# GpSimd normalises the softmax rows with one scalar per partition: four operations a step in place of two

## The chip, the core and the metric

The kernel runs on one core of a Trainium2 chip. The metric is the device time of one execution in microseconds (us), the median over several runs. Engines are named as in the profile: PE (TensorE; PEld is its weight load), DVE (VectorE), ACT (ScalarE), POOL (GpSimd) and SP (the queue that issues the DMAs here).

## What is computed

Two residual layers over x of shape (16, 256, 256), 4096 tokens of width 256, in float32.

```
# layer 0: attention, 16 heads of 64, one shared key/value head and one null key
xn = ln(x);  q = l2norm(xn @ Wq) * q_scale;  k = l2norm(xn @ Wk) * k_scale;  v = xn @ Wv
sim = 8 * q @ [k_null, k]^T + [null_bias, rel_pos_bias];  causal and given mask
attn = softmax(sim, axis=-1)          # this division is what the change touches
x = x + ln((attn @ [v_null, v]) @ Wout) * g_out
# layer 1: mixture of experts, 8 routed (best 2 of a softmax) and 2 shared blocks
h_e = leaky(x @ w_gate[e]) * (x @ w_up[e])
x = x + x1_part + sum_e weight_e * (h_e @ w_down[e])
```

## The kernel before

The program is written engine by engine; the order of work on each engine is the order of the code, and semaphores tie the engines together. The 4096 tokens go in eight rounds of 512 (two sequences of 256). Rounds 1 to 6 are one loop body (`Fori`), the first and the last round are written out. In round r the attention of round r is interleaved with the experts of round r-1, so that PE always has matmuls of one or the other.

Attention of a round runs in 16 steps n of two heads each: groups g of four steps, of which each has half the heads of one sequence. For each pair of heads there are two query tiles of 128 rows: tile 1 sees 256 keys and tile 0 sees 128, each with one null key behind them, so the rows in SBUF are `T1[sl]` (257 columns a head) and `T0[sl]` (129 columns a head), with `sl = g % 2`. All of them are parts of one buffer that the profile calls `work`. What one step does, in the order of the data:

- PE, `score` (L1502 to L1519): mask product (L1512) and score products (L1517) into psS.
- DVE, `scores` (L1153 to L1170): adds the bias, writes T1 and T0 and their lowest values (L1161, L1167), and frees psS for the next `score`.
- ACT, `exps` (L752 to L763): exponentials with the row sums `den` (L757, L761).
- DVE, `rdens` (L1140 to L1143): `rden = 1 / den`, one step later in DVE's order.
- POOL, the change (L591 to L595): waits for `rden_done`, multiplies T1's two heads by their reciprocals (L592) and T0's two heads by theirs (L594). Each is one `tensor_tensor` over both heads, the reciprocals read as a second tensor, broadcast along the row. The second one counts `norm_done` up.
- PE, `turn` (L1521 to L1539), three steps behind `score` (`TURN_LAG`): waits for `norm_done`, transposes T1 (L1528) and T0 (L1535) into psT, which ACT (L769) and DVE (L1176) copy out. `value` (L1553, L1556) follows five steps behind.

POOL has other work in the same queue: in eight of the 16 steps `weigh` (L606) multiplies an expert's hidden tile H by its token weights Wb ahead of the step's two operations; at step 9 a small power (L573) for the next round's first layer norm; at the ends of a round powers for other norms (L578, L581, L598).

DVE has two pieces of the next round's layer norm between its steps: at step 8 `norm_stats` (L846, L850, and L853, a `tensor_scalar` of four elements), and at step 11, just behind `rdens(10)`, `norm_x`: four `tensor_scalar` of 128x256 on `xin` (L858), each with a mean and a reciprocal deviation per partition. They stand ahead of `turned` (L1176) and of the next step's `scores`.

`stand` (L95 to L98) puts an instruction of its own behind a wait, so that the wait doesn't sit on the first of several operations.

Of the kernel before, what the change touches and what calls it, by code (L numbers as in the profile page):

```python
# [7 lines left out]
ALU = mybir.AluOpType  # L8
# [9 lines left out]
P = 128  # L18
B, N, D = 16, 256, 256
# [66 lines left out]
def need(eng, ev, r, c):  # L86


    value = ev.at(r, c)
    if isinstance(value, int) and value <= ev.base:  # L90
        return
    eng.wait_ge(ev.sem, value)


def stand(eng, waited):  # L95


    eng.sem_inc(waited, 1)  # L98
# [21 lines left out]
def attention_moe(nc, x, condT, condR, mask, wq, wkv, wout, wgu, wdown, wt, wgT, gnorm,  # L120
# [8 lines left out]
    with ExitStack() as ctx:  # L129
        def sb(name, shape, dt=F32):  # L130
            return ctx.enter_context(nc.sbuf_tensor(name, shape, dt))
# [4 lines left out]
        def events(name, per, base=0):  # L136
            return Events(ctx.enter_context(nc.semaphore(name)), per, base)
# [43 lines left out]
        T1 = [work[:, i * GH * (N + 1):(i + 1) * GH * (N + 1)].rearrange("p (h j) -> p h j", h=GH)  # L181
              for i in range(2)]
        T0 = [work[:, 2 * GH * (N + 1) + i * GH * (P + 1):2 * GH * (N + 1) + (i + 1) * GH * (P + 1)]
              .rearrange("p (h j) -> p h j", h=GH) for i in range(2)]
        low = [sb(f"low{i}", [P, 2, GH]) for i in range(2)]
        den = [sb(f"den{i}", [P, 2, GH]) for i in range(2)]
        rden = [sb(f"rden{i}", [P, 2, GH]) for i in range(2)]
# [199 lines left out]
        norm_done = events("norm_done", ALL)  # L387
# [20 lines left out]
        down_ps = events("down_ps", TILES)  # L408

        waited = ctx.enter_context(nc.semaphore("waited"))  # L410
        waited_sp = ctx.enter_context(nc.semaphore("waited_sp"))
        PRE_SMALL = 16 * 8

# [4 lines left out]
        def scale_q(eng, r, t, done):  # L418

            need(eng, rq_done, r, t + 1)  # L420
            need(eng, qs_done, r, t + 1)
            q3 = qs[t].rearrange("p (h d) -> p h d", h=HEADS)
            eng.tensor_tensor(q3, q3, rq[:, t, :].unsqueeze(2).to_broadcast([P, HEADS, DH]), ALU.mult) \  # L423
                .then_inc(done.sem, 1)
# [126 lines left out]
        @block.gpsimd  # L551
        def _(pool):
            pool.sem_inc(hw_done.sem, hw_done.base)
            pool.memset(ident[:], 0.0).then_inc(pre_p.sem, 1)
            pool.memset(neghalf[:], -0.5).then_inc(pre_p.sem, 1)
            pool.iota(posi[:], pattern=[[-P, 2]], base=N - 1, channel_multiplier=-1).then_inc(pre_p.sem, 1)
            pool.iota(iota8i[:], pattern=[[1, E]], base=0, channel_multiplier=0).then_inc(pre_p.sem, 1)
            pool.wait_ge(pre_p.sem, 4)
            pool.affine_select(out=ident[:], in_=ident[:], compare_op=ALU.not_equal, fill=1.0, base=0,
                               pattern=[[-1, P]], channel_multiplier=1).then_inc(pre_p.sem, 1)  # L560
            pool.wait_ge(pre_p.sem, 5)
            pool.memset(flip[:], 0.0).then_inc(flip_set.sem, 1)
            pool.wait_ge(flip_set.sem, 1)
            pool.affine_select(out=flip[:], in_=flip[:], compare_op=ALU.not_equal, fill=1.0, base=1 - P,
                               pattern=[[1, P]], channel_multiplier=1).then_inc(flip_set.sem, 1)

            def prologue_pow(k, out_, in_):
                pool.wait_ge(pre_v.sem, k)
                pool.tensor_tensor(out_, in_, neghalf[:, 0:out_.shape[-1]], ALU.pow).then_inc(pre_p.sem, 1)

            def norm_x(r):
                need(pool, ln_var, r, 1)
                pool.tensor_tensor(rstd[:], ve[:], neghalf[:, 0:TILES], ALU.pow).then_inc(rstd_done.sem, 1)  # L573

            def attention(r, moe, following):

                need(pool, kss_done, r, 1)
                pool.tensor_tensor(rk[:], kss[:], neghalf[:, 0:TILES], ALU.pow).then_inc(rk_done.sem, 1)  # L578
                for t in range(TILES):
                    need(pool, qss_done, r, t + 1)  # L580
                    pool.tensor_tensor(rq[:, t, :], qss[:, t, :], neghalf[:], ALU.pow).then_inc(rq_done.sem, 1)  # L581
                    if t < POOL_TILES:
                        scale_q(pool, r, t, qn_pool)
                for n in range(ALL):
                    g, st = n // STEPS, n % STEPS
                    sl, hs = g % 2, slice(2 * st, 2 * st + 2)
                    if moe is not None and n in WEIGH_AT:
                        weigh(moe, WEIGH_AT[n])
                    if n == NORM_AT + 1 and following is not None:
                        norm_x(following)  # L590
                    need(pool, rden_done, r, n + 1)  # L591
                    pool.tensor_tensor(T1[sl][:, hs, :], T1[sl][:, hs, :], rden[sl][:, 1, hs].unsqueeze(2)  # L592
                                       .to_broadcast([P, 2, N + 1]), ALU.mult)
                    pool.tensor_tensor(T0[sl][:, hs, :], T0[sl][:, hs, :], rden[sl][:, 0, hs].unsqueeze(2)  # L594
                                       .to_broadcast([P, 2, P + 1]), ALU.mult).then_inc(norm_done.sem, 1)  # L595
                for t in range(TILES):
                    need(pool, y_var, r, t + 1)
                    pool.tensor_tensor(rstd2[:, t:t + 1], ve2[:, t:t + 1], neghalf[:, 0:1],  # L598
                                       ALU.pow).then_inc(rstd2_done.sem, 1)

            def weigh(m, k):

                e = ORDER[k]
                need(pool, h_done, m, k + 1)
                need(pool, wb_in[e % WB_RING], m, 16 * (e // WB_RING + 1))
                pool.tensor_tensor(H[:, k % H_RING, :], H[:, k % H_RING, :], Wb[:, e % WB_RING, :], ALU.mult) \  # L606
                    .then_inc(hw_done.sem, 1)

            prologue_pow(V_VAR0, prs, pve)
            norm_x(0)  # L610
            prologue_pow(V_NSS, nrs, nss)
            prologue_pow(V_VAR1, prs, pve)
            attention(0, None, 1)
            with pool.Fori(1, ROUNDS - 1) as r:
                attention(r, r - 1, r + 1)
            attention(ROUNDS - 1, ROUNDS - 2, None)
            for k in range(SHARED, BLOCKS):
                weigh(ROUNDS - 1, k)
# [1120 lines left out]
```

## Time and profile before

| | us |
|---|---|
| median of 3 runs (1069.21 to 1070.3) | 1070.17 |
| the profiled execution's own time | 1068.73 |
| span of the profiled execution | 1066.9 |
| PE busy in it | 1011.4 (95%) |
| DVE busy | 725.8 (68%) |
| ACT busy | 541.0 (51%) |
| POOL busy | 438.6 (41%) |
| chain that ended last: PE | 70% |
| the same chain: DVE | 15% |
| the same chain: POOL | 0% |

The span is from the first to the last instruction of the profiled execution; the 1.8 us between it and that execution's own time lie around it. A share of busy time is an average over rounds and says nothing of who waits for whom; the chain of waits names, from the last instruction backwards, what released each step.

### The profile page before, as it was taken

Reading aid. Unit: us, or ns where it says so; the run is one execution under the profiler, and the core shown is the slowest. Engines: PE = TensorE matmul, PEld = TensorE weight load, DVE = VectorE, ACT = ScalarE, POOL = GpSimd, SP = SyncE. Lnnn points to the kernel's source line nnn. Section 1 sums busy time; section 2 is a strip of 40 time slices with the busy share of each in tenths; the row PEclk is TensorE's granted clock in tenths of the full one; section 3 lists DMA queues with packets and bytes.
Section 4 is the critical chain, followed back from the end, with each engine's and each line's share of the span. In section 5 each row is a group of like instructions: output and inputs, shape, how many; then the busy total and the mean of one; then the engine's idle time right before and its main releaser. Section 6 shows DMA issues by size and latency. Waiting matters only on the chain.

```text
span 1066.9 us, 22567 instructions
## 1 busy us (share of the span) xinstructions
PE 1011.4 (95%) x7300; PEld 823.6 (77%) x7300; DVE 725.8 (68%) x2497; ACT 541.0 (51%) x1596; POOL 438.6 (41%) x422
## 2 busy tenths in 40 slices
PE   3877999999999999999999999999999999999998
PEld 2765877878787887878777787787878788787877
DVE  8889487665867558665677647766586755866543
ACT  3598256652565435663456515665256643566220
POOL 1644254441454333642535515444145433354212
PEclk9999999999999999999999999999999999999999
DMA  5326423111132013311132212311113210221043
GB/s 198 73 77 209 138 69 121 51 60 62 61 110 89 36 47 100 100 61 61 42 114 77 69 42 72 119 49 62 62 61 110 89 37 29 96 103 62 36 133 105
DMA packets 41004, 87.79 MB, mean 82 GB/s; under 512 B 4193, under 2 KB 19041, under 8 KB 40625
## 3 DMA queue, kind: packets, MB, share of 16 engines
q1 hardware_dynamic: 39920, 83.57, 23.9%
q10 hardware_dynamic: 960, 2.62, 0.7%
q8 instruction: 73, 1.20, 0.5%
q14 instruction: 51, 0.41, 0.1%
HBM read 76.57 MB, written 9.60 MB: 81 GB/s over the span
## 4 chain that ended last, share of the span: by engine, by line
PE 70%; DVE 15%; issue 6%; ACT 3%; DVEq 0%; POOL 0%; ACTq 0%; POOLq 0%
PE psY L1647 13%; PE psS L1517 6%; PE psO L1553 5%; PE psG L71 5%; PE psG L69 5%; PE psG L70 5%; PE psT L1528 5%; PE psS L1512 3%; PE psS L69 2%; PE psS L71 2%; PE psS L70 2%; PE psT L1535 2%; PE psO L1556 2%; DVE work L423 2%; PE psT L69 2%
## 5 line engine op out<-in xcount | busy, mean ns | idle before, releaser
L592 POOL TENSOR_TENSOR work<-work,rden 128x514 f32<-128x514 f32 x128 | 134.2, 1049 | 328.6 <-DVE rden L1143 328.1
L1647 PE MATMUL psY<-Wd,H 128*128 128x256 f32 x640 | 171.7, 397 | 0.0
L757 ACT ACTIVATE work<-work,low 128x257 f32<-128x257 f32 x256 | 128.5, 504 | 63.5 <-DVE low L1161 63.5
L69 PE MATMUL psG<-x1T_hi,Wgu 128*128 128x512 f32 (+1 forms) x292 | 134.6, 461 | 3.5 <-ACT leaky L801 1.9
L1647 PEld LDWEIGHTS psY<-Wd,H 128*128 128x128 f32 x640 | 111.6, 189 | 28.1 <-issue 14.4
L1161 DVE CUSTOM_DVE_ANT_0 work<-psS,bias,null_s 128x256 f32<-128x256 f32 x256 | 113.1, 478 | 22.3 <-PE psS L1517 19.4
L1257 DVE SCALAR_TENSOR_TENSOR leaky<-leaky 128x512 f32<-128x512 f32 x80 | 55.4, 692 | 93.3 <-ACT leaky L801 93.3
L71 PE MATMUL psG<-x1T_lo,Wgu 128*128 128x512 f32 (+1 forms) x292 | 114.7, 393 | 0.0
L70 PE MATMUL psG<-x1T_hi,Wgu 128*128 128x512 f32 (+1 forms) x292 | 113.7, 389 | 0.0
L581 POOL TENSOR_TENSOR rq<-qss,neghalf 128x16 f32<-128x16 f32 x32 | 97.5, 3049 | 34.4 <-DVE qss L1137 34.4
L761 ACT ACTIVATE work<-work,low 128x129 f32<-128x129 f32 x256 | 99.4, 390 | 0.0
L606 POOL TENSOR_TENSOR H<-H,Wb 128x512 f32<-128x512 f32 x64 | 83.3, 1302 | 35.2 <-DMA Wb<-wscr 22.7
L769 ACT ACTIVATE PTs<-psT 128x512 f32<-128x512 f32 x128 | 75.6, 590 | 40.3 <-PE psT L1528 40.3
L749 ACT ACTIVATE qT_hi<-psO 128x256 fp32r<-128x256 f32 x112 | 42.9, 383 | 99.9 <-PE psO L1556 99.1
L598 POOL TENSOR_TENSOR rstd<-ve,neghalf 128x1 f32<-128x1 f32 x32 | 17.4, 545 | 171.9 <-DVE ve L1102 171.9
L1267 DVE TENSOR_TENSOR H<-psG,leaky 128x512 f32<-128x512 f32 x75 | 51.6, 689 | 49.7 <-PE psG L71 48.6
L1528 PE MATMUL psT<-ident,work 128*128 128x128 f32 x512 | 78.0, 275 | 6.9 <-ACT PTs L769 6.1
L1517 PE MATMUL psS<-KB_hi,qT_hi 64*128 64x256 f32 (+1 forms) x512 | 83.1, 317 | 0.0
L1528 PEld LDWEIGHTS psT<-ident,work 128*128 128x128 f32 x512 | 62.2, 140 | 24.4 <-issue 9.2
L594 POOL TENSOR_TENSOR work<-work,rden 128x258 f32<-128x258 f32 x128 | 79.4, 620 | 0.0
L1167 DVE CUSTOM_DVE_ANT_0 work<-psS,bias,null_s 128x128 f32<-128x128 f32 x256 | 79.0, 345 | 0.0
L1553 PE MATMUL psO<-PTs,kvs 128*64 128x256 f32 x448 | 73.0, 405 | 0.1
(264 smaller groups left out, 2567.6 us busy)
## 6 DMA issues: line engine op xcount, KB each, us to landing
Wgu<-wexp SPq DMA_DIRECT2D x80, 512.0 KB, 3.4
Wb<-wscr SPq DMA_DIRECT2D x64, 256.0 KB, 3.6
wexp<-Wgu SPq DMA_DIRECT2D x10, 512.0 KB, 2.9
xres<-in_x SPq DMA_DIRECT2D x8, 512.0 KB, 4.0
xin<-in_x SPq DMA_DIRECT2D x7, 512.0 KB, 4.1
out<-work SPq DMA_DIRECT2D x7, 512.0 KB, 3.2
H<-in_wgu SPq DMA_DIRECT2D x10, 256.0 KB, 3.5
bias<-bscr SPq DMA_DIRECT2D x4, 512.0 KB, 6.2
```

What stands on the lines that cost most here:

```text
L69: te.matmul(dst, a_hi, b_hi, start=start, stop=False)
L70: te.matmul(dst, a_lo, b_hi, start=False, stop=False)
L71: return te.matmul(dst, a_hi, b_lo, start=False, stop=stop)
L581: pool.tensor_tensor(rq[:, t, :], qss[:, t, :], neghalf[:], ALU.pow).then_inc(rq_done.sem, 1)
L592: pool.tensor_tensor(T1[sl][:, hs, :], T1[sl][:, hs, :], rden[sl][:, 1, hs].unsqueeze(2) .to_broadcast([P, 2, N + 1]), ALU.mult)
L757: act.activation(T1[sl][:, h, :], T1[sl][:, h, :], ACT.Exp, scale=-1.0, bias=low[sl][:, 1, h:h + 1], accum_out=den[sl][:, 1, h:h + 1])
L761: last = act.activation(T0[sl][:, h, :], T0[sl][:, h, :], ACT.Exp, scale=-1.0, bias=low[sl][:, 0, h:h + 1], accum_out=den[sl][:, 0, h:h + 1])
L1161: ins = dve.tensor_tensor_reduce(T1[sl][:, h, 0:N], psS[:, i, 0:N], bias[:, h0 + h, :], 1.0, null_s[:, 2 * bb + 1, h0 + h:h0 + h + 1], ALU ...
L1517: mm = te.matmul(psS[:, i, first:first + keys_], qT[a][half, p, q1:q1 + P], KB[b][half, bb, 0:keys_], start=False, stop=(first == N and b ...
L1528: mm = te.transpose(psT[:, 0, (2 * i + j) * P:(2 * i + j + 1) * P], T1[sl][:, 2 * s + i, j * P:(j + 1) * P], ident[:])
L1553: te.matmul(bank[i * DH:(i + 1) * DH, 0:N], kvs[:, 2 * bb, DH:2 * DH], PT[n % 2][:, i, 0:N], start=True, stop=False)
L1647: mm = te.matmul(psY[:, t // 2, (t % 2) * D:(t % 2 + 1) * D], H[:, k % H_RING, t * P:(t + 1) * P], Wd[:, ORDER[k], :], start=(k == 0 and t ...
```

## The change

In each of the 128 steps POOL multiplies the rows of one head at a time, with the reciprocal as a scalar per partition: T1's two heads, then T0's two heads. That is four `tensor_scalar` in place of two `tensor_tensor`. They write the same elements in the same order of tiles, and the last one counts `norm_done`. A `stand` with a semaphore of its own (`waited_pool`) goes between the wait and the first of them. No other engine's code changes, and `weigh`, the powers and all waits stay where they are.

```
         waited = ctx.enter_context(nc.semaphore("waited"))
+        waited_pool = ctx.enter_context(nc.semaphore("waited_pool"))
         waited_sp = ctx.enter_context(nc.semaphore("waited_sp"))
...
                     need(pool, rden_done, r, n + 1)
-                    pool.tensor_tensor(T1[sl][:, hs, :], T1[sl][:, hs, :], rden[sl][:, 1, hs].unsqueeze(2)
-                                       .to_broadcast([P, 2, N + 1]), ALU.mult)
-                    pool.tensor_tensor(T0[sl][:, hs, :], T0[sl][:, hs, :], rden[sl][:, 0, hs].unsqueeze(2)
-                                       .to_broadcast([P, 2, P + 1]), ALU.mult).then_inc(norm_done.sem, 1)
+                    stand(pool, waited_pool)
+                    for tile, T in ((1, T1), (0, T0)):
+                        for h in (2 * st, 2 * st + 1):
+                            last = pool.tensor_scalar(T[sl][:, h, :], T[sl][:, h, :], rden[sl][:, tile, h:h + 1], None,
+                                                      ALU.mult)
+                    last.then_inc(norm_done.sem, 1)
```

## Rows read from the trace of the kernel before

**Rows 1.** The page, costliest groups: xcount | busy us, mean ns | idle before, releaser.

```profile
L592 POOL TENSOR_TENSOR work<-work,rden 128x514 f32<-128x514 f32 x128 | 134.2, 1049 | 328.6 <-DVE rden L1143 328.1
L594 POOL TENSOR_TENSOR work<-work,rden 128x258 f32<-128x258 f32 x128 | 79.4, 620 | 0.0
L606 POOL TENSOR_TENSOR H<-H,Wb 128x512 f32<-128x512 f32 x64 | 83.3, 1302 | 35.2 <-DMA Wb<-wscr 22.7 <-DVE H L1267 12.4
```

**Rows 2.** POOL's instructions grouped by line: busy us, mean ns; idle before.

```profile
L598 POOL TENSOR_TENSOR rstd<-ve,neghalf 128x1 f32<-128x1 f32 x32 | 17.4, 545 | 171.9 <-DVE ve L1102 171.9
L573 POOL TENSOR_TENSOR rstd<-ve,neghalf 128x4 f32<-128x4 f32 x8 | 8.1, 1010 | 1.4 <-DVE ve L853 1.4
L559 POOL TENSOR_SCALAR_AFFINE_SELECT ident<-ident 128x128 f32<-128x128 f32 x1 | 0.3, 294 | 0.2 <-POOL iota8i L557 0.2
L554 POOL MEMSET ident<- 128x128 f32 x1 | 0.2, 205 | 0.4 <-POOLq L1729 0.4
L1729 POOL MEMSET const-uint8-127<- 128x1 uint8 x1 | 0.1, 103 | 0.0
```

**Rows 3.** Timeline of POOL, round 3, step 14: start, us, instruction.

```profile
482.53 1.28 POOL L606 TENSOR_TENSOR H<-H,Wb 128x512 f32<-128x512 f32 x1
483.89 1.04 POOL L592 TENSOR_TENSOR work<-work,rden 128x514 f32<-128x514 f32 x1
484.89 0.62 POOL L594 TENSOR_TENSOR work<-work,rden 128x258 f32<-128x258 f32 x1
```

**Rows 4.** Timeline, same place: step 13 on POOL, step 14's turn on PE.

```profile
480.95 1.04 POOL L592 TENSOR_TENSOR work<-work,rden 128x514 f32<-128x514 f32 x1 [2.65 <-DVE rden L1143]
...
487.51 0.66 PE L1528 MATMUL psT<-ident,work 128*128 128x128 f32 x4
```

**Rows 5.** Timeline, end of round 0: step 15 on POOL and its turn.

```profile
110.80 0.62 POOL L594 TENSOR_TENSOR work<-work,rden 128x258 f32<-128x258 f32 x1
111.64 0.55 PE L1528 MATMUL psT<-ident,work 128*128 128x128 f32 x3
```

**Rows 6.** Timeline of DVE and POOL, round 3, DVE's step 11, POOL's step 10.

```profile
466.51 0.18 DVE L1143 RECIPROCAL rden<-den 128x4 f32<-128x4 f32 x1
466.60 0.38 DVE L858 TENSOR_SCALAR xin<-xin,mv,rstd 128x256 f32<-128x256 f32 x1
466.76 1.12 POOL L592 TENSOR_TENSOR work<-work,rden 128x514 f32<-128x514 f32 x1 [2.72 <-DVE rden L1143]
466.89 1.14 DVE L858 TENSOR_SCALAR xin<-xin,mv,rstd 128x256 f32<-128x256 f32 x1
467.85 0.66 POOL L594 TENSOR_TENSOR work<-work,rden 128x258 f32<-128x258 f32 x1
467.95 0.70 DVE L858 TENSOR_SCALAR xin<-xin,mv,rstd 128x256 f32<-128x256 f32 x1
468.57 0.40 DVE L858 TENSOR_SCALAR xin<-xin,mv,rstd 128x256 f32<-128x256 f32 x1
```

**Rows 7.** Timeline of DVE: the same four with POOL idle, and colliding, as one row.

```profile
13.82 1.38 DVE L858 TENSOR_SCALAR xin<-xin,mv,rstd 128x256 f32<-128x256 f32 x4
466.60 2.38 DVE L858 TENSOR_SCALAR xin<-xin,mv,rstd 128x256 f32<-128x256 f32 x4
```

**Rows 8.** Timeline of PEld, round 3, the mask product's load at three steps.

```profile
465.82 0.10 PEld L1512 LDWEIGHTS psS<-MK,pick_bf 64*128 64x128 bf16 x2 [0.17 <-issue]
470.91 0.12 PEld L1512 LDWEIGHTS psS<-MK,pick_bf 64*128 64x128 bf16 x2 [0.44 <-issue]
475.74 0.10 PEld L1512 LDWEIGHTS psS<-MK,pick_bf 64*128 64x128 bf16 x2 [0.17 <-issue]
```

**Rows 9.** Timeline, round 0: an earlier hole; the collision and what follows.

```profile
56.89 0.34 PE L1512 MATMUL psS<-MK,pick_bf 64*128 64x384 bf16 x2 [1.64 <-DVE low L1167]
...
91.88 2.38 DVE L858 TENSOR_SCALAR xin<-xin,mv,rstd 128x256 f32<-128x256 f32 x4
96.19 0.12 PEld L1512 LDWEIGHTS psS<-MK,pick_bf 64*128 64x128 bf16 x2 [1.34 <-DVE low L1161]
101.49 0.48 DVE L1161 CUSTOM_DVE_ANT_0 work<-psS,bias,null_s 128x256 f32<-128x256 f32 x1 [0.94 <-PE psS L1517]
```

**Rows 10.** Windows: PE, PEld, DVE, ACT, POOL busy (count), PEclk, DMA share, GB/s.

```profile
97.30:100.70 3.40, 3.40 (x20) 2.37 (x20) 3.03 (x13) 3.19 (x14) 1.95 (x3) 0.51 0.65 231
```

**Rows 11.** Line L853: ns min/median/max; its place in round 3; PEld behind it.

```profile
L853 DVE TENSOR_SCALAR ve<-mv x8: 169/1090/1096, 11.0 to 831.9; 128x4 f32<-128x4 f32 x8
...
451.58 1.27 POOL L606 TENSOR_TENSOR H<-H,Wb 128x512 f32<-128x512 f32 x1
...
451.77 1.09 DVE L853 TENSOR_SCALAR ve<-mv 128x4 f32<-128x4 f32 x1
...
455.98 0.10 PEld L1512 LDWEIGHTS psS<-MK,pick_bf 64*128 64x128 bf16 x2 [0.17 <-issue]
```

## The prediction

> **What bounds the kernel now.** I read the page first: PE is busy for 95% of the span and has 70% of the chain of waits, POOL has none of it. Then POOL's own rows: ahead of L592 it is idle for 328 us in total, waiting for DVE's reciprocals, and both operations of a step take 1.05 and 0.62 us [rows 1]. So POOL waits for the others. Next the timeline, for how long each result lies before PE takes it. Over the 128 steps I set the end of L594 against the start of the transposes of that step (L1528). In the loop's rounds the least gap is at step 14: POOL is done at 484.89 + 0.62 = 485.51 and PE starts at 487.51 [rows 3, 4], 2.0 us later; in the other steps of these rounds the gap is 3 to 8 us. Only the last step of round 0 is close, 111.42 against 111.64, 0.22 us [rows 5]. A shorter operation on POOL gains nothing there.
>
> The one place where POOL's operation costs time is DVE. In its step 11 DVE issues the four `norm_x` operations right behind `rdens(10)`, which also sets POOL's next step off, so they start together. With POOL idle the four take 1.38 us [rows 7]; here they take 2.38, because the second takes 1.14 in place of 0.38 and the third 0.70 [rows 6]: each stands still until the POOL operation that began before it is about 0.2 us from its end. This is so in all seven rounds that have a following one. DVE's next `scores` then comes late, psS is freed late, and PE's mask product starts after 0.44 us of idle time where the steps before and after have 0.17 [rows 8]. In rounds 1 to 6 the other mask products from step 4 on wait 0.17 or 0.22 us, so the 0.27 us are PE's, in each of the six. In round 0 the hole is 1.34 us [rows 9], of which the collision can have made its whole 1.0 us, since the chain of waits there runs through L858, DVE's copy and `scores`, without a break.
>
> The Trainium skill, "SBUF — State Buffer", section "Who interferes with whom", says that DVE and GpSimd share one pair of SBUF ports, that it is an exclusive lock for the whole of an instruction, and that a DVE operation in a two-port mode (a float32 `tensor_scalar` within SBUF can be one) is the kind that is blocked. The trace agrees: L858 is blocked, 0.38 to 1.14 us.
>
> **The price of the new operations.** No `tensor_scalar` on POOL is in the trace. From L592 and L594, (1.049 - 0.620) / (514 - 258) = 1.68 ns an element and 0.187 us for an operation. L606, whose second tensor isn't broadcast, comes to (1.302 - 0.187) / 512 = 2.18 ns. With one tensor or none to read it is less: the fill of 128 columns against one column gives (205 - 103) / 127 = 0.80 ns, and the select over 128 columns takes 0.294 us [rows 2], which is 0.187 + 128 x 0.83. I take the new ones as like the select, the nearest kind (one tensor in, one out): 0.187 + 257 x 0.83 = 0.40 us and 0.187 + 129 x 0.83 = 0.29 us. Four of them, less 0.04 us of overlap between neighbours (L594 starts 1.00 us behind L592, which takes 1.04 [rows 3]), are 1.38 - 0.12 = 1.26 us a step, against 1.63 now. The floor is the fill's cost, 0.10 us and 0.80 ns: 0.9 us a step. The ceiling takes the fixed part of the powers, (1010 - 545) / 3 = 155 ns an element, so 0.39 us an operation [rows 2], and L606's 2.18 ns: 0.95 and 0.67 us, 3.1 us a step. `stand` adds one instruction to the queue; the time from the end of L1143 to the start of L592 is 466.76 - 466.69 = 0.07 us [rows 6], and I give it no more than that again, in front of a gap of 2 us: nothing on PE.
>
> The Trainium skill, "GPSIMD Engine Reference", section 7, speaks against four small operations: each read command costs about 102 cycles that don't overlap with the one before. Were the scalar's read such a command, that would be an estimate of 85 ns an operation at the page's 1.2 GHz, and a step would take 1.6 us, as much as now; no row of this trace shows it.
>
> **The gain on PE.** POOL's step shrinks by 0.37 us, 47 us over the 128 steps, and nobody was waiting: 0. What counts is the collision. Now DVE's second operation has to let L592 pass (0.75 us) and its third L594 (0.3). With four short ones they take turns: POOL's first (0.40) starts at 466.76 and lets DVE go at about 467.0, where DVE wanted 466.9; the same again at the third and the fourth, each 0.1 to 0.15. The four then take 1.38 + 0.35 = 1.7 us, 0.65 less than now. By the estimate of 85 ns more they'd take about 1.9, still 0.5 less.
> - Rounds 1 to 6: PE's hole closes by 0.27 us, and no more than that, since the rest is the usual 0.17: 6 x 0.27 = 1.6 us.
> - Round 0: DVE is on the chain there, so PE comes 0.6 us earlier: 0.6 us.
> - `weigh` starts 0.37 us earlier in six steps. At step 8 it blocks DVE's tiny L853 for 0.9 us (1.09 where 0.17 is the price with POOL idle), from 451.77 on [rows 11]; the block shrinks to 0.55. Nothing on PE: its hole behind it is the usual 0.17 us at 455.98 [rows 11], so the wait is covered by PE's matmuls. If that cover were gone, 0.37 us a round would be to gain.
> - The last round has no `norm_x`: 0.
>
> The sum is -2.2 us. Against the profiled execution's 1068.73 that is 1066.5; the median of the runs stands 1.44 above that execution, so I expect 1070.17 - 2.2 = 1068.0 us.
>
> **The rivals.**
> - *Nothing moves.* The new operations take 0.6 us (the 1.68 ns an element of L592 for 257 columns, and 0.187), a step 1.9 us. DVE then waits for POOL's first three in turn, 0.35 + 0.4 + 0.2, as long as now. Or PE's 0.27 us is taken up by the wait that comes next (ACT's or DVE's copies of psT). For it: no row has the operation. Against it: the select and the fill. 1070.2 us.
> - *The clock holds in round 0.* From 97.3 to 100.7 us TensorE's granted clock is 0.51 of full speed, so its lower level, 1.2 GHz [rows 10], and just before that PE idled for the 1.34 us of the hole [rows 9]. With a hole of 0.7 us it may not fall. PE's 3.4 us would take half, and at 101.49 DVE waited 0.94 us for it [rows 9], so it gives 0.9 to 1.7 us more: 1066.7 us. For it: a hole of 1.64 us ahead of 56.9 us [rows 9] didn't bring the clock down, so the two aren't tied one to one, and a little less idle time may be enough. Against it: the same row shows that the idle time of one hole isn't the whole of it.
> - *Slower: the fixed part decides.* There are 512 starts in place of 256. If each costs the powers' 0.39 us and the elements L606's rate, a step takes 3.1 us. DVE's second, third and fourth operation wait 0.65 + 0.65 + 0.4 us, 0.7 more than now, and PE has that in all seven rounds: +5 us. And at step 14 POOL ends at 480.95 + 3.1 + 1.36 (`weigh`, 482.53 to 483.89) + 3.1 = 488.5, where PE starts at 487.51 [rows 3, 4]: 1.0 us in each of seven rounds and some 1.5 in round 0: +8. Together 1083 us. It decides from 2.6 us a step on at PE ((487.51 - 482.31) / 2), and at the collision from about 0.6 us for the first operation. For it: nothing but the lack of a row; the select and L594 both have 0.19 us fixed.
> - *POOL doesn't let DVE in between its four.* Then DVE waits once, for the burst: 1.26 + 0.08 - 0.13 - 0.2 = 1.0 us, the same as now: no change, and with a dearer operation a little slower, 0.2 to 0.4 us a round for each 0.3 us. Against it: between L592 and L594 DVE did get in [rows 6].
>
> That the change doesn't do what it says can be excluded: the compiled queue has four TENSOR_SCALAR where it had two operations, 128 times.
>
> **How the numbers follow.** A measurement of this kernel can tell 0.2% from nothing, 2.1 us, and the forecast stands right at that edge. The forecast's mechanism with the clock as it is: 0.56, of which I give 0.34 to more than 2.1 us and 0.22 to less. The clock holds as well: 0.10, faster. Nothing moves, by either way: 0.23. Slower by over 2.1 us: 0.11. That makes 0.44 faster, 0.45 the same, 0.11 slower. The range goes from 1065.5 (the clock's 1.7 us and the collision's 2.2 together with half a us of scatter) to 1072.0, which takes in no change (1070.2) and the collision made worse by some 0.3 us a round; the full price of the slower rival is left out.
>
> **What would show it.** In the profile after: POOL's rows at about 400 and 290 ns, 256 each; POOL busy down by 45 to 50 us; the four L858 in about 1.7 us in place of 2.38; the mask product's idle time of 0.17 us at the step behind them; in round 0 the hole of 1.34 at about 0.7. The prediction is wrong if the new operations take over 0.6 us, if L858 takes as long as before, or if PE's hole closes and the time doesn't follow.

## The result and the profile after

The changed kernel takes 1083.31 us (median of 4 runs, 1082.84 to 1084.1) against 1069.69 us of the kernel before in the same comparison (4 runs, 1068.92 to 1070.3). The ratio is 1.0133, with a 95% interval of 1.0117 to 1.0148: slower by 13.6 us. The span of the profiled execution goes from 1066.9 to 1081.8 us, by 14.9; the two profiled executions themselves took 1068.73 and 1083.6 us. Behind the change's place all lines of this kernel have moved down by three, so L1528 of before is L1531 here, L1647 is L1650, and so on; L592 and L594 have become L596, and `weigh` is L609.

From the page after: the engines, and the chain of waits by engine.

```profile
PE 1010.7 (93%) x7300; PEld 822.9 (76%) x7300; DVE 724.8 (67%) x2497; ACT 540.9 (50%) x1596; POOL 620.0 (57%) x678
...
PE 66%; DVE 11%; POOL 8%; issue 7%; ACT 2%; DVEq 0%; POOLq 0%; ACTq 0%
```

POOL is busy for 620.0 us in place of 438.6, and its share of the chain has gone from 0 to 8%. PE does the same work in a longer span. POOL's instructions grouped by line, with the two shapes of L596 apart (xcount | busy us, mean ns | idle before):

```profile
L596 POOL TENSOR_SCALAR work<-work,rden 128x257 f32<-128x257 f32 x256 | 237.6, 942 | 180.5 <-DVE rden L1146 180.4
L596 POOL TENSOR_SCALAR work<-work,rden 128x129 f32<-128x129 f32 x256 | 156.4, 625 | 0.0
```

An operation takes 942 or 625 ns. The forecast had 400 and 290, its ceiling 950 and 670. From one shape to the other that is (942 - 625) / 128 = 2.48 ns an element and 0.305 us fixed, and four in a row take 3.02 us, where the old pair took 1.63. PE's waits for POOL in the trace after (engine, tile and line that waits, releaser: total us, count, longest):

```profile
PE psT L1531 <- POOL work L596: 10.2, 11, 1.3
PE psY L1650 <- POOL H L609: 7.5, 7, 1.1
```

The same view of before puts 0.7 us of PE's idle time down to POOL's rows, in two waits of round 0. But these rows had been ready for 2.8 and 3.7 us by then, so PE waited for something else there. For `weigh` PE never waited.

Nearly the whole loss is in two waits. The lower row is PE's down product waiting for `weigh`, 7 times: one place in seven rounds, and the prediction doesn't have it. **In the timeline of before** (start, us, instruction), round 3, steps 1 and 2:

```profile
425.85 1.04 POOL L592 TENSOR_TENSOR work<-work,rden 128x514 f32<-128x514 f32 x1 [3.56 <-DVE rden L1143]
...
427.42 1.28 POOL L606 TENSOR_TENSOR H<-H,Wb 128x512 f32<-128x512 f32 x1
427.47 0.60 PE L1528 MATMUL psT<-ident,work 128*128 128x128 f32 x4
429.12 0.70 PE L1647 MATMUL psY<-Wd,H 128*128 128x256 f32 x2
431.49 0.60 PE L1528 MATMUL psT<-ident,work 128*128 128x128 f32 x4
```

`weigh` stands in POOL's queue behind the whole of step 1 and ended at 427.42 + 1.28 = 428.70; the down product took its tile H at 429.12. So there were 0.42 us of slack, and a step, counted up to the start of `weigh`, had room to grow from 427.42 - 425.85 = 1.57 to 2.0 us, no further. **The same place after:**

```profile
430.83 3.02 POOL L596 TENSOR_SCALAR work<-work,rden 128x257 f32<-128x257 f32 x4 [2.14 <-DVE rden L1146]
432.33 0.60 PE L1531 MATMUL psT<-ident,work 128*128 128x128 f32 x4
433.82 1.27 POOL L609 TENSOR_TENSOR H<-H,Wb 128x512 f32<-128x512 f32 x1
435.14 1.13 PE L1650 MATMUL psY<-Wd,H 128*128 128x256 f32 x4 [1.09 <-POOL H L609]
437.49 0.60 PE L1531 MATMUL psT<-ident,work 128*128 128x128 f32 x4
```

`weigh` ends at 435.09, the down product starts at 435.14 after 1.09 us of idle time, and the two turns around it are 437.49 - 432.33 = 5.16 us apart, where they were 431.49 - 427.47 = 4.02: 1.14 us.

The other wait is at step 14 of the same round; [rows 3, 4] are its place before. The timeline after, POOL and then PE:

```profile
486.79 3.02 POOL L596 TENSOR_SCALAR work<-work,rden 128x257 f32<-128x257 f32 x4 [1.18 <-DVE rden L1146]
489.77 1.28 POOL L609 TENSOR_TENSOR H<-H,Wb 128x512 f32<-128x512 f32 x1
491.02 3.03 POOL L596 TENSOR_SCALAR work<-work,rden 128x257 f32<-128x257 f32 x4
...
494.10 0.66 PE L1531 MATMUL psT<-ident,work 128*128 128x128 f32 x4 [0.81 <-POOL work L596]
```

POOL works from 486.79 to 494.05 without a gap, and PE waits. The upper row of the waits has 11 of this kind: six at step 14 of the loop's rounds, two each at steps 14 and 15 of the last round and of round 0, and one at step 9 of round 0. There POOL's step 8, the small power and step 9 follow each other without a gap from 86.59 us on, step 9 is done at 94.54, and the transposes start right behind it:

```profile
91.13 8.57 POOL L596 TENSOR_SCALAR work<-work,rden 128x257 f32<-128x257 f32 x10
...
94.60 0.66 PE L1531 MATMUL psT<-ident,work 128*128 128x128 f32 x4 [1.14 <-POOL work L596]
```

And the collision, which answers to [rows 7, 8]:

```profile
472.59 1.85 DVE L861 TENSOR_SCALAR xin<-xin,mv,rstd 128x256 f32<-128x256 f32 x4
472.88 3.05 POOL L596 TENSOR_SCALAR work<-work,rden 128x257 f32<-128x257 f32 x4 [1.30 <-DVE rden L1146]
...
476.63 0.10 PEld L1515 LDWEIGHTS psS<-MK,pick_bf 64*128 64x128 bf16 x2 [0.17 <-issue]
```

`norm_x` takes 1.85 us in place of 2.38 though POOL is busy beside it from 0.29 us on, and PE's hole is 0.17 in place of 0.44: this is what the prediction wanted to see, with operations more than twice as long as it thought.

**Where the 14.9 us lie.** I set the start of each of the 128 turns (L1531) against that of before (L1528), and took the growth of the difference from one to the next. Elsewhere it is 0.1 us or less.

| | rounds 1 to 6, each | last round | round 0 |
|---|---|---|---|
| between the turns of steps 0 and 1 (`weigh`) | +1.13 | +1.16 | 0 |
| at step 10's turn (collision) | -0.28 | none | -2.1, over steps 10 to 13 |
| at the turns of steps 14 and 15 | +0.88 | +0.78, +1.39 | +0.97, +1.39 |
| before step 10: first turn, step 9's turn (wait for POOL) | 0 | 0 | +0.53, +0.61 |
| sum | 10.3 in all | 3.3 | 1.4 |

### The profile page after: what moved, and what is told of

Same layout as the page of the kernel before. It is cut to its first block, busy times and chain, and to the rows that moved or that the text cites. A ratio compares the mean times of both kernels' runs of the same rounds, so it can differ in the third digit from the quotient of the medians.

```text
span 1081.8 us, 22951 instructions
## 1 busy us (share of the span) xinstructions
PE 1010.7 (93%) x7300; PEld 822.9 (76%) x7300; DVE 724.8 (67%) x2497; ACT 540.9 (50%) x1596; POOL 620.0 (57%) x678
## 4 chain that ended last, share of the span: by engine, by line
PE 66%; DVE 11%; POOL 8%; issue 7%; ACT 2%; DVEq 0%; POOLq 0%; ACTq 0%
PE psY L1650 11%; POOL work L596 7%; PE psS L1520 5%; PE psG L71 5%; PE psG L69 5%; PE psG L70 5%; PE psO L1556 4%; PE psT L1531 4%; PE psS L69 2%; PE psS L70 2%; PE psS L71 2%; PE psS L1515 2%; PE psT L69 2%; PE psT L71 2%; PE psT L70 2%
## 5 line engine op out<-in xcount | busy, mean ns | idle before, releaser
L596 POOL TENSOR_SCALAR work<-work,rden 128x257 f32<-128x257 f32 (+1 forms) x512 | 389.9, 783 | 180.5 <-DVE rden L1146 180.4
L1650 PE MATMUL psY<-Wd,H 128*128 128x256 f32 x640 | 171.7, 397 | 7.5 <-POOL H L609 7.5
L1650 PEld LDWEIGHTS psY<-Wd,H 128*128 128x128 f32 x640 | 111.7, 189 | 35.9 <-issue 15.6
L1260 DVE SCALAR_TENSOR_TENSOR leaky<-leaky 128x512 f32<-128x512 f32 x80 | 62.3, 779 | 100.2 <-ACT leaky L804 100.2
L609 POOL TENSOR_TENSOR H<-H,Wb 128x512 f32<-128x512 f32 x64 | 82.7, 1293 | 35.5 <-DMA Wb<-wscr 25.3
L1531 PE MATMUL psT<-ident,work 128*128 128x128 f32 x512 | 77.6, 274 | 17.2 <-POOL work L596 10.2
L1531 PEld LDWEIGHTS psT<-ident,work 128*128 128x128 f32 x512 | 61.9, 140 | 35.4 <-POOL work L596 16.2
L1179 DVE COPY PTs<-psT 128x256 f32<-128x256 f32 x128 | 52.0, 406 | 32.5 <-PE psT L1538 17.4
```

The costliest lines, as they stand in the source:

```text
L596: last = pool.tensor_scalar(T[sl][:, h, :], T[sl][:, h, :], rden[sl][:, tile, h:h + 1], None, ALU.mult)
L1531: mm = te.transpose(psT[:, 0, (2 * i + j) * P:(2 * i + j + 1) * P], T1[sl][:, 2 * s + i, j * P:(j + 1) * P], ident[:])
L1650: mm = te.matmul(psY[:, t // 2, (t % 2) * D:(t % 2 + 1) * D], H[:, k % H_RING, t * P:(t + 1) * P], Wd[:, ORDER[k], :], start=(k == 0 and t ...
```

## The experiments

All times are compared with runs of the kernel before on the same chip, 1068.57 to 1068.88 us. The rival here is that a scalar read from SBUF is what makes each operation dear; my theory is that it is the kind of operation, and that POOL's lateness at two places does the rest.

**Prices by themselves.** Behind the last `weigh` of before, POOL does three of each of ten operations on scratch rows, 257 and 129 elements; the rest of the kernel is as it was.

```
+for i in range(3):
+    last = pool.tensor_scalar(dst[:, 257 * i:257 * i + 257], src[:, 0:257], s1, None, ALU.mult)
...
+for i in range(3):
+    last = pool.tensor_scalar(dst[:, 257 * i:257 * i + 257], src[:, 0:257], 0.5, None, ALU.mult)
...
+for i in range(3):
+    last = pool.tensor_copy(dst[:, 257 * i:257 * i + 257], src[:, 0:257])
...
+for i in range(3):
+    last = pool.tensor_tensor(dst[:, 257 * i:257 * i + 257], src[:, 0:257], s1.to_broadcast([P, 257]), ALU.mult)
...
```

> The kernel before, with 30 operations on POOL behind its last weigh, three of a kind, on 257 and 129 columns: tensor_scalar with a scalar per partition, tensor_scalar with a constant, tensor_copy, tensor_tensor with a broadcast second input, tensor_tensor with a full second input. They write a tile that nobody reads any more. Theory A (the scalar read per partition is what is dear): the constant form and the copy take 0.40 and 0.29 us, the pointer form 0.94 and 0.62. Theory B (tensor_scalar on POOL is a slow operation whatever its scalar): both forms take 0.94 and 0.62, the copy 0.4 and 0.3. Theory C (L596 is long because of what runs beside it in the kernel): the pointer form is shorter here than 0.94 and 0.62. Broadcast tensor_tensor by the rows of before: 0.187 + 257 x 1.68 ns = 0.62 and 0.40; full: 0.187 + 257 x 2.18 ns = 0.75 and 0.47.

POOL's rows at the end of this kernel (the last number ahead of the second bar is the mean in ns):

```profile
L625 POOL TENSOR_SCALAR xin<-x,neghalf 128x257 f32<-128x257 f32 x3 | 2.8, 936 | 0.0
L633 POOL TENSOR_SCALAR xin<-x 128x257 f32<-128x257 f32 x3 | 2.5, 857 | 0.1
L657 POOL TENSOR_TENSOR xin<-x 128x257 f32<-128x257 f32 x3 | 2.1, 727 | 0.1
L629 POOL TENSOR_SCALAR xin<-x,neghalf 128x129 f32<-128x129 f32 x3 | 1.8, 612 | 0.1
L649 POOL TENSOR_TENSOR xin<-x,neghalf 128x257 f32<-128x257 f32 x3 | 1.7, 611 | 0.1
L637 POOL TENSOR_SCALAR xin<-x 128x129 f32<-128x129 f32 x3 | 1.5, 538 | 0.1
...
L653 POOL TENSOR_TENSOR xin<-x,neghalf 128x129 f32<-128x129 f32 x3 | 1.1, 398 | 0.1
L641 POOL COPY xin<-x 128x257 f32<-128x257 f32 x3 | 1.1, 402 | 0.1
L645 POOL COPY xin<-x 128x129 f32<-128x129 f32 x3 | 0.8, 297 | 0.1
```

L625 and L629 have the scalar in SBUF, L633 and L637 a constant: 79 and 74 ns between them, for either length. Here at the end, where DVE has a single group of operations left beside them, they take 936 and 612 ns, as good as the 942 and 625 of the changed kernel, so what runs beside them there isn't the reason either. The elements cost (857 - 538) / 128 = 2.49 ns in a `tensor_scalar` even with the constant, (611 - 398) / 128 = 1.66 in a `tensor_tensor` whose second tensor is a broadcast, (402 - 297) / 128 = 0.82 in a copy. So the pointer is a small part; the kind of operation decides, and the copy's 402 and 297 are just what the forecast had put down for the `tensor_scalar`. The Trainium skill, "GPSIMD Engine Reference", section 7 (about 102 cycles for a read command that doesn't overlap), gave the prediction's estimate of 85 ns, if the scalar's read is such a command; the two differences are near it, and no run shows that this is their cause. The same page, section 4.1, has one-input operations roughly at line rate; here that holds for the copy and not for `tensor_scalar`, which is dearer than the two-input operation, and the measurement decides. The kernel's one execution took 1081.91 us, with this extra work at its end.

**Four `tensor_tensor`.** The change's order, one head at a time, with the old kind of operation.

```
-                            last = pool.tensor_scalar(T[sl][:, h, :], T[sl][:, h, :], rden[sl][:, tile, h:h + 1], None,
-                                                      ALU.mult)
+                            last = pool.tensor_tensor(T[sl][:, h, :], T[sl][:, h, :], rden[sl][:, tile, h:h + 1]
+                                                      .to_broadcast([P, T[sl].shape[-1]]), ALU.mult)
```

> The changed kernel with each of its four operations as a tensor_tensor over one head, the reciprocal broadcast. Theory A (the kind of operation sets the time, not the number of instructions): 0.62 and 0.40 us each, 1.92 us a step, which is under 2.6 at step 14 and adds 0.3 to the queue ahead of weigh, where 0.4 is free: the time of before, 1069 to 1071. Rival (number of starts): as the change, 1083.

Measured: 1066.33 us, ratio 0.9978 (0.9968 to 0.9987). In its trace, POOL's rows by shape, and round 3's collision:

```profile
L596 POOL TENSOR_TENSOR work<-work,rden 128x257 f32<-128x257 f32 x256 | 152.3, 617 | 293.9 <-DVE rden L1146 293.9
L596 POOL TENSOR_TENSOR work<-work,rden 128x129 f32<-128x129 f32 x256 | 98.0, 404 | 0.0
...
466.36 2.05 DVE L861 TENSOR_SCALAR xin<-xin,mv,rstd 128x256 f32<-128x256 f32 x4
466.63 2.05 POOL L596 TENSOR_TENSOR work<-work,rden 128x257 f32<-128x257 f32 x4 [2.43 <-DVE rden L1146]
...
470.40 0.10 PEld L1515 LDWEIGHTS psS<-MK,pick_bf 64*128 64x128 bf16 x2 [0.17 <-issue]
```

The gain of the forecast comes from cutting the operations in two, with no cheaper step: four of them take 1.91 us as a rule and 2.05 us here, where the old pair took 1.62 and 1.75. `norm_x` still takes 2.05 us, 0.33 less than before, and yet PE's hole is closed (-0.28 a round in the turns). So of the 1.0 us by which the collision made DVE late in a loop round, only the last 0.33 reached PE.

**`weigh` one step earlier.** The changed kernel, with the first `weigh` of a round (k = 2) ahead of POOL's step 1 instead of its step 2.

```
-WEIGH_AT = {2: 2, 3: 3, 4: 4, 6: 5, 8: 6, 10: 7, 12: 8, 14: 9}
+WEIGH_AT = {1: 2, 3: 3, 4: 4, 6: 5, 8: 6, 10: 7, 12: 8, 14: 9}
```

> The changed kernel with the first weigh of the eight (k = 2) one step earlier, ahead of POOL's step 1 in place of step 2. Theory: PE's first down product of that block waits 1.1 us for it in each of seven rounds, because it stands behind a 3.0 us step; moved, all of this goes: 1083.3 - 7 x 1.13 = 1075.4, and the wait at step 14 stays. Rival (the 1.13 us come from DVE's leak, which is blocked for 0.87 us by the same weigh): the time stays at 1082 to 1083, or the wait comes back elsewhere.

Measured: 1075.8 us, 1.0071 (1.0051 to 1.0091). In round 3 `weigh` now ends at 426.11 + 1.28 = 427.39, and the down product, in the second row, has no wait in front of it:

```profile
426.11 1.28 POOL L609 TENSOR_TENSOR H<-H,Wb 128x512 f32<-128x512 f32 x1
...
431.48 1.13 PE L1650 MATMUL psY<-Wd,H 128*128 128x256 f32 x4
```

The +1.13 is gone in all seven rounds and the steps of 0.88 stay. Against the changed kernel's 1.0133 this is 0.0062 of the ratio back, 6.6 us, and 8.0 in the turns: one edit of one number takes back about half of the loss.

**The old operations in steps 13 to 15.** The changed kernel elsewhere.

```
-                    for tile, T in ((1, T1), (0, T0)):
+                    if n < 13:
+                        for tile, T in ((1, T1), (0, T0)):
...
+                    else:
+                        pool.tensor_tensor(T1[sl][:, hs, :], T1[sl][:, hs, :], rden[sl][:, 1, hs].unsqueeze(2)
...
```

> The changed kernel with the old two operations in the last three steps of each round (13 to 15). Theory: PE's wait at the turn of step 14 goes (6 x 0.88 + 0.78 + 1.39 in the loop's rounds and the last one, 0.97 + 1.39 in round 0, together 9.8 us), the wait for the first weigh stays: 1083.3 - 9.8 = 1073.5. Rival (the end of a round is late because POOL has fallen behind all along, not because of its last steps): it goes by less than half of that, to 1078 or more.

Measured: 1073.58 us, 1.0049 (1.0032 to 1.0066). In the turns nothing is left at steps 14 and 15, and the +1.13 stands.

**Both of these edits together.** The changed kernel with

```
+WEIGH_AT = {1: 2, 3: 3, 4: 4, 6: 5, 8: 6, 10: 7, 12: 8, 14: 9}
...
+                    if n < 13:
...
```

> The changed kernel with the first weigh one step earlier and the old two operations in steps 13 to 15. Theory: the two waits on POOL were all that the change cost, and what stays is its gain where DVE and POOL collide (6 x 0.28 us in the loop's rounds and 1.1 in round 0): 1083.3 - 7.9 - 9.8 = 1065.6, some 4 us under before. Rival (there is a third cost spread over the steps): 1070 or more.

Measured: 1065.89 us, 0.9974 (0.9962 to 0.9985). So with the dear operation in 104 of 128 steps (416 of 512 operations) the kernel is faster than before: a long step costs nothing where POOL has slack. These two waits are the loss; the one at step 9 of round 0 is still there (1.14 us, +0.61 in the turns), and the next turn takes it back (-1.34).

**The new operations in one step alone.** The kernel before, with the four `tensor_scalar` at POOL's step 10, the one beside `norm_x`.

```
+                    if n == 10:
+                        for tile, T in ((1, T1), (0, T0)):
...
+                    else:
...
```

> The kernel before with the four new operations in POOL's step 10 alone, the one that runs beside DVE's four norm_x operations. Theory (the tensor_scalar form holds the shared resource for less time, though it is longer): the four take 1.85 us in place of 2.38, PE's hole closes by 0.27 us in six rounds and by more in round 0: 1067 to 1068. Rival (the gain came from POOL being late there, not from the form): no gain, 1069.7.

Measured: 1066.02 us, 0.9972 (0.9963 to 0.9981). `norm_x` takes 1.58 or 1.86 us, depending on the round.

**The collision taken away by DVE's order.** The kernel before, with `norm_x` ahead of `rdens(10)`.

```
+                    if following is not None and n == NORM_AT + 3:
+                        norm_x(following)
                     if 1 <= n <= ALL:
                         rdens(r, n - 1)
-                    if following is not None:
-                        if n == NORM_AT:
-                            norm_stats(following)
-                        if n == NORM_AT + 3:
-                            norm_x(following)
+                    if following is not None and n == NORM_AT:
+                        norm_stats(following)
```

> The kernel before with DVE's norm_x ahead of rdens in its step 11, so that POOL, which rdens sets off, is idle while the four run; no tensor_scalar on POOL at all. Theory: the collision goes whole, the four take 1.38 us, PE's hole closes to 0.17: 1.6 us in the loop's rounds and 1 to 2 in round 0: 1066.5 to 1067.5. Rival (DVE's own 1.4 us make the hole): the hole stays near 0.4 us and the time within 0.5 us of before.

Measured: 1065.78 us, 0.9972 (0.9961 to 0.9983). POOL starts behind the four, which are back at the price of [rows 7]:

```profile
465.27 1.38 DVE L858 TENSOR_SCALAR xin<-xin,mv,rstd 128x256 f32<-128x256 f32 x4
...
466.82 1.05 POOL L592 TENSOR_TENSOR work<-work,rden 128x514 f32<-128x514 f32 x1 [4.01 <-DVE rden L1142]
...
469.40 0.10 PEld L1511 LDWEIGHTS psS<-MK,pick_bf 64*128 64x128 bf16 x2 [0.17 <-issue]
```

The collision is gone entirely here, and the time is that of the versions in which `norm_x` still takes 1.6 to 2.05 us. PE gets 0.28 us a loop round in all of them: they close the same hole. So their gains shouldn't add up; no run has two of them together.

**A step between the two thresholds.** The new operation for T1, the old one for T0: 2.4 us a step. The prediction's threshold at step 14 was 2.6 us, that of `weigh` by the rows above is 2.0.

```
+                    for h in (2 * st, 2 * st + 1):
+                        pool.tensor_scalar(T1[sl][:, h, :], T1[sl][:, h, :], rden[sl][:, 1, h:h + 1], None, ALU.mult)
                     pool.tensor_tensor(T0[sl][:, hs, :], T0[sl][:, hs, :], rden[sl][:, 0, hs].unsqueeze(2)
```

> The changed kernel with tensor_scalar for T1's two heads and the old single operation for T0's: 2 x 0.94 + 0.62 = 2.4 us a step. Theory (thresholds: PE waits at step 14 from 2.6 us a step on, and for the first weigh from 2.05 on, where 0.42 us were free): no wait at step 14, 0.4 us for the weigh in seven rounds, the collision's gain of 0.28 in six: 1069.7 + 2.8 - 1.7 = 1070.8, between 1069.5 and 1072. Rival (the cost goes with the time added on POOL, 13.6 us for 1.4 us a step): 1069.7 + 13.6 x 0.8 / 1.4 = 1077.5.

Measured: 1071.84 us, 1.0029 (1.0017 to 1.0041). In the turns: +0.54 at `weigh` in seven rounds, nothing at step 14 in the loop's rounds (round 0 +0.13 and +0.79 at its end, the last round +0.38), -0.28 at step 10. Both thresholds hold.

```profile
429.54 1.27 POOL L608 TENSOR_TENSOR H<-H,Wb 128x512 f32<-128x512 f32 x1
...
430.87 1.13 PE L1649 MATMUL psY<-Wd,H 128*128 128x256 f32 x4 [0.46 <-POOL H L608]
```

**The old pair done twice.** The kernel before, with each `tensor_tensor` done once more into a scratch tile first, 3.2 us a step. (The scratch operations also wait for POOL's own step before.)

```
+                    pool.tensor_tensor(scratch[:, :, 0:N + 1], T1[sl][:, hs, :], rden[sl][:, 1, hs].unsqueeze(2)
+                                       .to_broadcast([P, 2, N + 1]), ALU.mult)
+                    pool.tensor_tensor(scratch[:, :, N + 1:], T0[sl][:, hs, :], rden[sl][:, 0, hs].unsqueeze(2)
+                                       .to_broadcast([P, 2, P + 1]), ALU.mult)
```

> The kernel before, each step's two operations done twice: first into a scratch tile that nobody reads, then in place. A step takes about 3.25 us, all of it tensor_tensor. Theory (the time a step takes on POOL, in two waits of PE, is the whole cost, whatever the kind): the wait for the first weigh is 1.13 + 0.22 in seven rounds (9.5), step 14 is 0.88 + 0.44 in six (7.9), the last round's end 2.8, round 0 some 3, and the long broadcast operations hold DVE's norm_x for 0.7 us more than now in seven rounds (4.9): 28 us, 1097, between 1090 and 1100. Rival (there is something in the tensor_scalar form that costs time beside its length): clearly less than that, under 1085.

Measured: 1099.05 us, 1.0278 (1.0263 to 1.0294). In rounds 1 to 7 the waits sit at the same two places, with no `tensor_scalar` in POOL's steps; in round 0, which grows by 8.3 us, they come at steps 3 to 9 as well:

```profile
PE psT L1537 <- POOL work L603: 22.3, 18, 2.1
...
PE psY L1656 <- POOL H L615: 9.1, 7, 1.3
```

A loop round has +1.36 at `weigh` and +1.27 at step 14. The collision, though, differs from the changed kernel: `norm_x` takes 3.23 us in three loop rounds, which cost 0.85 us each, and 2.38 in the other three, which cost nothing. So a longer burst on POOL can hurt DVE if it is made of `tensor_tensor`, as the slower rival had it; made of `tensor_scalar`, in the changed kernel, it didn't in any of the seven rounds (1.57 to 1.85 us).

**`stand` alone** in the kernel before.

```
                     need(pool, rden_done, r, n + 1)
+                    stand(pool, waited_pool)
```

> The kernel before with the stand of the change alone: one more sequencer instruction a step, behind the wait. Theory: it is some tens of ns on POOL in front of a gap of 2 us or more: nothing, within 0.7 us of before. Rival (the stand lets DVE's norm_x start first and so is behind part of the gain at the collision): 1 us or more faster.

Measured: 1068.51 us, 0.9999 (0.999 to 1.0008). It costs nothing, as the prediction had it.

**More of the query scaling on POOL (two misses).** With the collision gone by DVE's order, POOL also scales the queries of token tile 3, in the second kernel of tiles 2 and 3, which DVE did; the idea was that POOL has time to spare and DVE is on PE's path at the start of a round.

```
-                    if t < POOL_TILES:
+                    if t in (0, 3):
                         scale_q(pool, r, t, qn_pool)
...
-                    if n == 0:
-                        scale_q(dve, r, 3, qn_done)
```

> The kernel with norm_x ahead of rdens (e7), and POOL instead of DVE scales the queries of tile 3. POOL is idle for 12 us there in each round, and DVE's 1.22 us stand in front of the second scores, for which PE's third mask product waits 1.26 us in each round. Theory (POOL's idle time ahead of step 0 is where it can help, unlike inside the steps): 1.05 us a round in rounds 1 to 7, 7.4 us: 1068.7 - 2.9 - 7.4 = 1058.4. Rival (PE's transposes of tile 3 then wait for POOL's powers and its 1.9 us): the gain is under 2 us, 1064 or more.

> As e11, with tile 2 on POOL as well, which takes 1.22 us from in front of the first scores, for which PE's second mask product waits 1.17 us. Theory: up to 1 us a round more in rounds 1 to 7, 1051.5. Rival (POOL's powers come late: tile 2's scaling pushes tile 3's power back by 1.9 us, and null_parts on DVE waits for that power): no gain over e11 or a loss.

Measured: 1078.66 us, 1.0097 (1.0074 to 1.012), and 1078.34 us, 1.0093 (1.0076 to 1.011). Both are slower where I expected 10 and 17 us to be won. Round 3 of the first, the POOL operation, a DVE operation of 32 elements beside it, and PE's first mask product; the last row is that small DVE operation in the kernel before, with POOL idle.

```profile
411.65 1.90 POOL L423 TENSOR_TENSOR work<-work,rq 128x1024 f32<-128x1024 f32 x1
411.78 1.82 DVE L1232 TENSOR_TENSOR wsel<-oh,score 128x32 f32<-128x32 f32 x1
...
415.59 0.34 PE L1509 MATMUL psS<-MK,pick_bf 64*128 64x384 bf16 x2 [1.52 <-DVE qT_lo L1118]
```

```profile
408.94 0.16 DVE L1235 TENSOR_TENSOR wsel<-oh,score 128x32 f32<-128x32 f32 x1
```

The operation takes 1.82 us in place of 0.16, the queries' low part comes later for it, and PE waits 1.52 us; each round is 1.1 to 1.5 us longer by its first turn. How much of the cost is this block wasn't tried apart: POOL's scaling itself, 1.90 us, also takes longer than DVE's of the same tile in the kernel before, 1.22.

## Why the prediction was wrong

**What failed first: the price of the new operations.** The step reads "I take the new ones as like the select, the nearest kind (one tensor in, one out)". A `tensor_scalar` on POOL costs 942 and 625 ns, the select's rate is that of a copy (0.82 ns an element), and so a step takes 3.02 us, not 1.26. The ceiling, 0.95 and 0.67 us, was right within 8 and 45 ns, by luck in part, since it was put together from 0.39 us fixed and 2.18 ns an element where 0.31 and 2.48 were measured. It should have weighed more: nothing in the rows told an arithmetic operation with one input from a move. The range left the ceiling's consequence out; the condition "wrong if the new operations take over 0.6 us" was met.

**What failed second: whose wait comes first when POOL is late.** The sum's term "nobody was waiting: 0" holds for a shorter step; with 3.02 us a step it became +8.0 us at `weigh` and +9.8 at steps 14 and 15. "`weigh` starts 0.37 us earlier in six steps" looks at `weigh` only for a shorter step, and the slower rival looks only at step 14. The slack of every consumer of POOL was needed: `weigh` at step 2 had 0.42 us, so PE waits there from 2.0 us a step, ahead of step 14's 2.6. From the start of the step before and the measured length it comes to 425.85 + 2.99 (from a step's start to `weigh` in the rows after, 433.82 - 430.83) + 1.27 = 430.11 against 429.12, 1.0 us; 1.13 was measured. The rest is that POOL's step starts 0.1 us later than before, seen from the turn beside it (432.33 - 430.83 = 1.50 us ahead of it, before 427.47 - 425.85 = 1.62).

**The slower rival: right in its sum, wrong in its parts.**

| | rival | measured |
|---|---|---|
| collision with `norm_x` | +5 | -1.7 in rounds 1 to 6, -2.1 around it in round 0 |
| steps 14 and 15 | +8 | +9.8 |
| `weigh` at step 2 | not in it | +8.0 |
| before step 10 in round 0 | not in it | +1.1 |
| together | +13: 1083 us | +14.9 in the traces, 1083.31 us |

Its agreement with the time is no proof of it. The -2.1 holds the collision and the clock: the stretch of [rows 10] at 1.2 GHz is gone, and one further ahead has come. Windows of the changed kernel, then of the one before, and last of the version with `weigh` one step earlier (PE, PEld, DVE, ACT, POOL busy, the granted clock, DMA share, GB/s):

```profile
45.00:60.00 15.00, 12.07 (x85) 9.74 (x86) 11.62 (x38) 8.73 (x27) 7.49 (x6) 0.89 0.73 225
97.30:100.70 3.40, 2.82 (x36) 2.15 (x32) 3.24 (x13) 3.40 (x13) 3.40 (x5) 1.00 0.70 242
...
45.00:60.00 15.00, 11.05 (x90) 9.04 (x92) 12.38 (x39) 10.09 (x29) 7.50 (x4) 1.00 0.81 228
...
97.30:100.70 3.40, 2.56 (x28) 1.97 (x28) 3.24 (x15) 3.40 (x13) 3.40 (x6) 1.00 0.83 284
```

So the rival of the clock that holds in round 0 was half right: in the changed kernel it holds at 97 us and falls before 60, and the first turn, at 62 us, comes 0.53 us later. In the versions with `weigh` earlier and with the old operations in steps 13 to 15 the granted clock is 1.00 throughout the first 110 us; their turns of steps 10 to 13 differ from before by the same -1.34, -0.41, -0.39 and +0.07 as the changed kernel's, and their first turns are 0.05 and 0.65 us earlier. So the last three, 0.7 us, go with the 1.2 GHz of [rows 10], and 1.34 belong to step 10, of which 0.61 only take back the wait at step 9 (with the new operations at step 10 alone, and no such wait, it is -0.80). The first turn moves by more than half a us without any 1.2 GHz ahead of it, so its +0.53 can't be put down to the clock alone. What makes the clock fall at one place or the other, or not at all, stays open.

**What was right.** PE bounds the kernel. That nobody gains by a shorter POOL step wasn't put to the test, since no run has one; before, the only transposes that began within 1 us of POOL's end were those of [rows 5]. The collision costs PE 0.27 us in each loop round, and splitting POOL's burst gives that back and no more: -0.28, 6 times, in the changed kernel too, and with nothing against it -2.4 and -2.8 us in the versions of four `tensor_tensor` and of DVE's order, where -2.2 was forecast. The clock isn't behind these two: among executions with a granted clock of 1.000 over the whole span, before took 1067.53 to 1067.95 us (four of them), four `tensor_tensor` 1065.68 to 1065.99 (three) and DVE's order 1065.02 and 1065.48. Round 0's term, 0.6 us, was the loose one: by step 10's turn DVE's order gains 1.02 us there and four `tensor_tensor` 0.33. `stand` is free. At step 14 the threshold of 2.6 us holds, and 0.88 us was lost where 1.0 was worked out. The rival in which 0.6 us operations bring nothing fell: at 617 and 404 ns the gain is whole.

## What to carry to other kernels

Before an operation on an engine gets longer, list every consumer of that engine with its slack, those that are queued behind it too, and work out the length at which each begins to wait; the first threshold counts, not the one that the change is about. A price for an operation that the trace lacks is worth one run: five kinds at two lengths were measured in one, behind POOL's last use. And where a fix brings a known wait to its floor, a second fix of the same wait has nothing left to bring, so take the one without side effects: here DVE's order (1065.78 us, 0.9972), the best version with no new operation, though the three others at 1065.9 to 1066.3 can't be told from it.

## What the runs showed of the hardware that I had not expected

- On POOL a float32 `tensor_scalar` (2.5 ns an element, 857 ns for 257 with a constant) is dearer than a `tensor_tensor` with a broadcast (1.66 ns, 611) and than one with two full tensors (727 for 257); a copy costs 402.
- A `tensor_scalar` on POOL holds DVE's `tensor_scalar` much less than a `tensor_tensor` does: `norm_x` takes 1.38 us alone, 1.57 to 1.86 beside four `tensor_scalar` (3.05 us), 2.05 beside four `tensor_tensor` (2.05 us), 2.38 beside two, up to 3.23 beside four large ones. The Trainium skill, "SBUF — State Buffer", section "Who interferes with whom", has the other engine blocked for the whole of the instruction that came first; beside `tensor_scalar` the trace doesn't agree.
- DVE holds POOL as well. In round 0 of the changed kernel a step of four `tensor_scalar` takes up to 4.00 us in place of 3.02; in step 8 (3.54 us) the third one takes 1.14 us in place of 0.61, beside a DVE `tensor_tensor` of 128x512 that takes its usual 0.68.
- The time of an execution goes with the granted clock over its whole span. Of the kernel before, the four executions at 1.000 took 1067.53 to 1067.95 us, the 34 at 0.998 1068.09 to 1069.74, and the five at 0.995 1070.11 to 1070.98: about 1 us from the first level to the second, where one stretch like that of [rows 10] lies in the span, and 3 us to the third.
- Small DVE operations can stand still for nearly the whole of a POOL operation: 1.82 us in place of 0.16 for 32 elements (L1232 above), with both inputs in SBUF. A larger one in the changed kernel, 0.69 us by itself, takes 1.56 beside `weigh` and costs nothing, since PE has no idle time behind it:

```profile
438.04 1.29 POOL L609 TENSOR_TENSOR H<-H,Wb 128x512 f32<-128x512 f32 x1
...
438.31 1.56 DVE L1260 SCALAR_TENSOR_TENSOR leaky<-leaky 128x512 f32<-128x512 f32 x1 [2.61 <-ACT leaky L804]
```
